# Decoder layer, gated delta rule: the output projection as three fp32r products of split halves

## The chip, the cores and the metric

One Trainium2 chip, one core of it. The time is device microseconds (us) of one execution of the whole program; lower is better.

## What is computed

A decoder layer on x of 16 batches x 128 positions x 256 features, float32. Its first part, a gated delta rule with 16 key heads and 32 value heads, takes most of the time, and its last lines are what the change touches:

```python
    o = o.transpose(1, 0, 2, 3)                   # output of the recurrence, B x S x 32 x 128
    og = o * jax.nn.silu(z)
    var = jnp.mean(og * og, axis=-1, keepdims=True)
    on = og * jax.lax.rsqrt(var + EPS) * norm_w
    return on.reshape(B, S, VAL_DIM) @ w_out      # 4096 x 256
...
    x = _layernorm(x + _L0_attn_ref(x, ...), axis=-1)
    x = _layernorm(x + _L0_xattn_ref(x, ctx_512, ctx_512), axis=-1)
    x = _layernorm(x + _L0_ffn_ref(x, ...), axis=-1)
```

## The kernel before

The recurrence is solved in closed form per batch and head. The work of the first part is cut into 64 steps: a step is one key head (so two value heads) and four batches, 8 pairs of batch and value head. One loop over n = 0 to 72 writes the instructions of all five engines, and it runs several stages of a software pipeline at once: stage 1 works on step n (projection of keys and queries, products of keys), the v stage on vn = n - 7, the third stage on m = n - 8 (the triangular inverse, deltas, outputs, gate), the fourth on k = n - 9 (norm, transpose and output projection). There is no scheduler: each engine runs what stands in its block in the order written, and counts of semaphores are all that ties the engines together. SP (SyncE) issues all transfers, in one order too.

What TensorE does in one pass of the loop, in order, with the lines of the profile: z_proj(m, 0) (L1326 to L1328 with 256 columns, fp32r); the 32x32 products u1 (L1504), which wait for the gate of the step before; q_norms (L1358); z_proj(m, 1); the small products L1517 and L1524; v_proj of vn, two banks (L1326 to L1328 with 512 columns); u2 of four pairs (L1537); the key products of step n (L1548, 4 of them, fp32); u2 and tt128 of the other four pairs (L1555 and L1456); on_tr(k, 0) and on_tr(k, 1), the eight transposes of the normed output into banks 4 and 5 (L1434); four more tt128 (L1456); out_proj(k, 0) and out_proj(k, 1) (L1451); deltas (L1469); kq_proj of n + 1 (L1326 to L1328 with 512 columns), which waits for the last convolution tap of v; the transposes of v (L1585); outputs (L1485).

VectorE, in the same pass: taps 2 and 3 of the convolution of keys and queries for step n (tap 1 stands at the end of the pass before; all are L897), the scalar of q_norms (L1131), a stretch of the inverse (L913 to L980), the taps 1 and 2 of v (L897), the four products of step n (L1100), tap 3 of v (L897), a stretch of the inverse, the diagonals (L1159), y_add(k), which adds the output projection out of banks 7 and 6 to Y (L1110), a stretch of the inverse, the two gates of m (L1115), tap 1 of n + 1. The 32x32 inverses are made for four steps together, in 41 operations; a generator hands them out in portions whose sizes the code sets (`pump(room)`). So the passes differ by n mod 4: in this text a pass is called of kind 0, 1, 2 or 3 by it. An inverse begins in a pass of kind 0 and ends in one of kind 3.

ScalarE: copies of u1 (L742), squares of the gated output (L688), SiLU of keys and queries (L748), copies L752 and L756, SiLU of z (L681), the copies v_tap3 with tap 0 of v (L669), the copies of u2 (L784, two halves), in kind 3 the copy of the inverse into another order (L794), on_T(k, 0) and on_T(k, 1), which bring the transposed normed output from banks 4 and 5 to the tile DL (L675), the copy L799, and later SiLU of v (L806), deltas (L812), kq_tap3 (L658) and v (L821). In kind 3 on_T(k, 0) stands before L794 and on_T(k, 1) behind it. GpSimd: the norm of step m, whose last instruction scales SZ (L578); then L554, the decay masks (L494, L498), the low halves of split weights (L472) and scale_wo, which multiplies w_out of a key head by the norm's weight (L485).

Projections from x are already made as three products of halves: a float32 operand is split into a high half, rounded to fp32r, and a low half, the rest (split_hi on ScalarE, split_lo on GpSimd), and high x high, high x low and low x high are added (`three`, L1326 to L1328). The output projection instead is one plain float32 product per pair:

```python
for b in range(2):
    for v in range(2):
        t = pe.matmul(ps(7 - i, b * 256, [[1, 256]]), at(on_buf(k), (4 * i + 2 * b + v) * 128, [[1, 128]]),
                      at(WO, (k // 4 % 2) * 512 + v * 256, [[1, 256]]), start=(v == 0), stop=(v == 1))
t.then_inc(sem["out_mm"], 1)
```

It shows as two instructions per product in the profile, 16 per step. Banks 4 and 5 are written in turn by z_proj, on_tr, deltas and the transposes of v. After the 64 steps come cross attention and the experts, by tables of steps; the output projections of the last two steps stand at their beginning.

## Time and profile before

| | us |
|---|---|
| median of 3 runs | 2288.58 |
| lowest and highest | 2284.19, 2304.11 |
| the profiled execution | 2284.63 |
| its span, first to last instruction | 2282.7 |

Rows of the profile give the start in us from the span's beginning, the duration, the engine, the line, the operation, what it writes and reads, how many instructions are merged, and in brackets the idle time of the engine before it with what ended that. PE is TensorE (PEld its weight loads), DVE VectorE, ACT ScalarE, POOL GpSimd. A merged row's duration reaches to the end of its last instruction, and instructions overlap a little, so the cost of a row to its engine is read from its start to the next row's start.

### The profile page before, as it was taken

What the parts mean: (1) busy time and instruction counts of PE and PEld (TensorE: products, weight loads), DVE (VectorE), ACT (ScalarE), POOL (GpSimd) and SP (SyncE); (2) the same over time, 40 slices, a digit from 0 to 9 for tenths busy, and PEclk for the clock granted to TensorE, in tenths of its full rate; (3) what the DMA queues carried; (4) which work ended last, traced back from release to release, by engine and by line L of the source; (5) the groups of instructions that cost most, each with busy time, mean ns of one, the idle gap of its engine ahead of it and who ended that gap; (6) DMA issues with size and microseconds to landing.
All of it is one profiled execution on the core that took longest, in us unless ns stands there. A gap on an engine that the chain in (4) does not pass through costs nothing.

```text
span 2282.7 us, 48904 instructions
## 1 busy us (share of the span) xinstructions
PE 2116.3 (93%) x18108; PEld 1754.0 (77%) x18108; DVE 1799.2 (79%) x3536; ACT 1508.3 (66%) x3585; POOL 858.5 (38%) x760
## 2 busy tenths in 40 slices
PE   4659999999999999999999999998888899999998
PEld 4448888888888888888888888887766466666677
DVE  6889797988979788897978989797324776767665
ACT  4536777767677777777777777775656766566632
POOL 1533344435344444434434443531333123223232
PEclk8769999999999999999999999999889999999999
DMA  3332223232232332223233222312143012221232
GB/s 76 92 71 48 74 51 80 55 70 66 49 86 47 72 63 62 66 57 82 42 76 74 48 67 59 74 34 55 56 130 132 1 47 93 102 93 59 90 135 97
DMA packets 274635, 161.54 MB, mean 71 GB/s; under 512 B 209352, under 2 KB 246752, under 8 KB 269280
## 3 DMA queue, kind: packets, MB, share of 16 engines
...
## 4 chain that ended last, share of the span: by engine, by line
PE 75%; DVE 11%; ACT 6%; issue 4%; DMA 2%; SPq 1%; POOL 1%; DVEq 0%; ACTq 0%; POOLq 0%
PE ps L1326 9%; PE ps L1451 9%; PE ps L1328 8%; PE ps L1327 8%; PE ps L1548 5%; PE ps L1485 5%; PE ps L1469 5%; PE ps L1704 4%; PE ps L1434 3%; PE ps L1358 2%; PE ps L1585 2%; PE ps L1504 2%; PE ps L1555 2%; ACT SC L844 1%; PE ps L1456 1%
## 5 line engine op out<-in xcount | busy, mean ns | idle before, releaser
L897 DVE SCALAR_TENSOR_TENSOR A<-ps,CW,A 128x508 f32<-128x508 f32 (+2 forms) x768 | 516.1, 735 | 115.7 <-ACT A L669 109.8
L571 POOL TENSOR_SCALAR SM<-SM 128x8 f32<-128x8 f32 x64 | 12.7, 198 | 891.8 <-ACT DL L688 891.8
L1451 PE MATMUL ps<-WO,DL 128*128 128x256 f32 x1008 | 243.4, 393 | 8.8 <-ACT TTF L799 8.8
L1326 PE MATMUL ps<-XH,WH 128*128 128x512 f32 x512 | 218.3, 426 | 25.5 <-DVE A L897 24.1
L1451 PEld LDWEIGHTS ps<-WO,DL 128*128 128x128 f32 x1008 | 189.1, 194 | 42.3 <-ACT DL L675 14.1
L1328 PE MATMUL ps<-XH,WL 128*128 128x512 f32 x512 | 205.1, 401 | 0.0
L1327 PE MATMUL ps<-XL,WH 128*128 128x512 f32 x512 | 204.5, 399 | 0.0
L688 ACT ACTIVATE DL<-SZ 128x128 f32<-128x128 f32 x512 | 152.3, 299 | 66.6 <-issue 42.0
L1115 DVE TENSOR_TENSOR SZ<-SZ,ps 128x512 f32<-128x512 f32 x128 | 86.2, 685 | 124.7 <-PE ps L1485 123.1
L844 ACT ACTIVATE SC<-ps,A 128x128 f32<-128x128 f32 x512 | 141.7, 386 | 51.9 <-DVE A L1231 51.3
L1100 DVE TENSOR_TENSOR BP<-ps,EB 128x512 f32<-128x512 f32 x256 | 158.3, 682 | 2.7 <-ACT EB L663 2.7
L1326 PE MATMUL ps<-WH,XH 128*128 128x256 f32 x512 | 156.7, 306 | 0.7 <-ACT VV L821 0.7
L1327 PE MATMUL ps<-WL,XH 128*128 128x256 f32 x512 | 145.5, 284 | 0.0
L1328 PE MATMUL ps<-WH,XL 128*128 128x256 f32 x512 | 145.2, 284 | 0.0
L494 POOL TENSOR_TENSOR EB<-EB,HJ 128x1024 f32<-128x1024 f32 x64 | 128.9, 2015 | 38.2 <-DMA EB<-decay_rows 38.2
L578 POOL TENSOR_TENSOR SZ<-SZ,SM 128x1024 f32<-128x1024 f32 x64 | 140.2, 2190 | 5.0
L1548 PE MATMUL ps<-A 128*128 128x256 f32 x512 | 133.9, 406 | 4.8 <-DVE SM L1131 3.4
L1326 PEld LDWEIGHTS ps<-XH,WH 128*128 128x128 f32 x512 | 99.1, 194 | 48.9 <-issue 15.4
L658 ACT ACTIVATE A<-ps,CW 128x512 f32<-128x512 f32 x128 | 86.3, 689 | 70.9 <-PE ps L1328 49.5
L1469 PEld LDWEIGHTS ps<-VV,TTF 128*128 128x128 f32 x1024 | 125.9, 194 | 4.9 <-ACT TTF L799 1.7
L1485 PE MATMUL ps<-DL,BP 128*128 128x128 f32 x1024 | 127.2, 278 | 0.7 <-DVE Y L1110 0.2
L1469 PE MATMUL ps<-VV,TTF 128*128 128x128 f32 x1024 | 126.5, 277 | 1.4 <-ACT TTF L799 1.4
...
## 6 DMA issues: line engine op xcount, KB each, us to landing
EB<-decay_rows SPq DMA_DIRECT2D x128, 256.0 KB, 4.8
...
x_blocks<-BP SPq DMA_DIRECT2D x256, 32.0 KB, 1.7
...
TTF<-tt_blocks SPq DMA_DIRECT2D x256, 32.0 KB, 1.9
...
```

What stands on the lines that cost most here:

```text
L578: pool.tensor_tensor(szp, szp, at(SM, C_RR, [[1, 8], [0, 128]]), ALU.mult).then_inc(sem["on"], 1)
L688: t = act.activation(at(DL, pr * 128, [[1, 128]]), at(SZ, (m % 2) * 1024 + pr * 128, [[1, 128]]), ACT.Square, accum_out=at(SM, C_SS + pr, ...
L844: t = act.activation(at(SC, i * 512 + h * 128, [[1, 128]]), ps(s_bank(a, i), h * 128, [[1, 128]]), ACT.Exp, bias=q(Q_MX + 4 * i + h, [[1, ...
L897: dve.scalar_tensor_tensor(acc, ps(i, 0, [[128, 4], [1, 128 - s]]), at(CW, tile * 4 + 3 - s, [[1, 1]]), acc, ALU.mult, ALU.add).then_inc(s ...
L1100: dve.tensor_tensor(slot(n, h * 1024 + v * 256, [[512, 2], [128, 2], [1, 128]]), ps(2 + h, 0, [[256, 2], [128, 2], [1, 128]]), at(EB, (n % ...
L1326: pe.matmul(out, sa, ma, start=(kt == 0), stop=False)
L1327: pe.matmul(out, sa, mb, start=False, stop=False)
L1328: return pe.matmul(out, sb_, ma, start=False, stop=(kt == 1))
L1451: t = pe.matmul(ps(7 - i, b * 256, [[1, 256]]), at(on_buf(k), (4 * i + 2 * b + v) * 128, [[1, 128]]), at(WO, (k // 4 % 2) * 512 + v * 256, ...
L1469: t = pe.matmul(ps(4 + i, j * 128, [[1, 128]]), at(TTF, pr * 128, [[1, 128]]), at(VV, pr * 128, [[1, 128]]), start=True, stop=True)
L1485: t = pe.matmul(ps(6 + i, j * 128, [[1, 128]]), slot(m, pr * 256 + 128, [[1, 128]]), at(DL, pr * 128, [[1, 128]]), start=True, stop=True)
L1548: t = pe.matmul(ps(2 + b // 2, (b % 2) * 256, [[1, 256]]), at(buf, b * 128, [[1, 128]]), at(buf, b * 128, [[512, 2], [1, 128]]), start=Tru ...
```

## The change

Four things are changed.

- out_proj becomes out_hi and out_lo. Of the transposed normed output, on_T on ScalarE writes the high half (fp32r, tile DLR, which lies on DL), and a new on_lo(k, i) on VectorE writes the rest into SZR (which lies on SZ): it reads bank 4 + i and DLR. TensorE makes 16 products with the high half (with the high and the low half of the weights) and then 8 with the low half.
- The weights are split once per key head: they are loaded into the slot of w_v in WR between two loads of w_v, scaled there by GpSimd, rounded by ScalarE (split_wo_hi) and their rest made by GpSimd (split_wo_lo), into a new tile WOR. Before, two slots of WO were filled by turns.
- on_tr(k, 0) stands before the key products instead of behind L1555, and on ScalarE on_T(k, 0) stands between the two copies of u2.
- Banks 4 and 5, and the next SiLU of z, are freed by on_lo and out_mm instead of on_T and on_tr.

```diff
                 def load_v(hk):
...
-                        sp.wait_ge(sem["lo_v"], hk)
+                        sp.wait_ge(sem["wo_lo"], hk)
...
                 def load_wo(hk):
-                    if hk >= 2:
-                        sp.wait_ge(sem["out_mm"], 2 * (4 * (hk - 2) + 3) + 2)
-                    sp.dma_start(at(WO, (hk % 2) * 512, [[256, 2], [1, 256]]),
+                    sp.wait_ge(sem["lo_v"], hk + 1)
+                    sp.dma_start(at(WR, W_V, [[256, 2], [1, 256]]),
...
-                    if 0 <= vn < NSTEP and vn % 4 == 1 and vn // 4 + 1 < HK:
-                        load_v(vn // 4 + 1)
...
+                    if n % 4 == 2 and 0 <= n // 4 - 1 < HK:
+                        load_wo(n // 4 - 1)
+                    if n % 4 == 0 and 0 < n // 4 - 1 < HK:
+                        load_v(n // 4 - 1)
...
+                def split_wo_lo(hk):
+                    pool.wait_ge(sem["wo_hi"], hk + 1)
+                    pool.tensor_tensor(at(WOR, 512, [[1, 512]]), at(WR, W_V, [[1, 512]]), at(WOR, 0, [[1, 512]]).bitcast(f32),
+                                       ALU.subtract).then_inc(sem["wo_lo"], 1)
...
+                def split_wo_hi(hk):
+                    act.wait_ge(sem["wo_scaled"], hk + 1)
+                    if hk:
+                        act.wait_ge(sem["out_mm"], 8 * hk)
+                    act.activation(at(WOR, 0, [[1, 512]]), at(WR, W_V, [[1, 512]]), ACT.Copy).then_inc(sem["wo_hi"], 1)
...
                     if s3:
-                        for i in range(2):
-                            act.wait_ge(sem["u2"], 2 * m + 1 + i)
-                            act.activation(at(U2, i * 256, [[1, 256]], 64, 64), ps(7, i * 256, [[1, 256]], 64, 64), ACT.Copy,
-                                           scale=-1.0).then_inc(sem["u2_sb"], 1)
+                        u2_copy(m, 0)
+                    if s4 and k < NSTEP - 1:
+                        on_T(k, 0)
+                    if s3:
+                        u2_copy(m, 1)
...
+                    if n % 4 == 0 and 0 <= n // 4 - 2 < HK:
+                        split_wo_hi(n // 4 - 2)
...
+                def on_lo(k, i):
+                    dve.wait_ge(sem["on_T"], 2 * k + 1 + i)
+                    dve.tensor_tensor(on_low(k, i * 512, 512), ps(4 + i), at(on_buf(k), i * 512, [[1, 512]]).bitcast(f32),
+                                      ALU.subtract).then_inc(sem["on_lo"], 1)
...
                     pump(1560)
+                    if s4 and k < NSTEP - 1:
+                        on_lo(k, 0)
                     if sv:
                         v_tap(vn, 1)
+                    if s4 and k < NSTEP - 1:
+                        on_lo(k, 1)
...
-                def out_proj(k, i):
+                def out_hi(k, i):
                     if k % 4 == 0 and i == 0:
-                        pe.wait_ge(sem["wo_scaled"], k // 4 + 1)
+                        pe.wait_ge(sem["wo_lo"], k // 4 + 1)
...
+                            for part in range(2):
+                                pe.matmul(ps(7 - i, b * 256, [[1, 256]]),
+                                          at(on_buf(k), (4 * i + 2 * b + v) * 128, [[1, 128]]),
+                                          at(WOR, part * 512 + v * 256, [[1, 256]]),
+                                          start=(b == 0 and v == 0 and part == 0), stop=False)
+
+                def out_lo(k, i):
+                    pe.wait_ge(sem["on_lo"], 2 * k + 1 + i)
+                    for b in range(2):
+                        for v in range(2):
+                            t = pe.matmul(ps(7 - i, b * 256, [[1, 256]]), on_low(k, (4 * i + 2 * b + v) * 128, 128),
+                                          at(WOR, v * 256, [[1, 256]]), start=False, stop=(b == 1 and v == 1))
                     t.then_inc(sem["out_mm"], 1)
+
+                def out_proj(k):
+                    out_hi(k, 0)
+                    out_hi(k, 1)
+                    out_lo(k, 0)
+                    out_lo(k, 1)
...
                     if m:
-                        pe.wait_ge(sem["on_T"], 2 * (m - 1) + 1 + i)
+                        pe.wait_ge(sem["on_lo"], 2 * (m - 1) + 1 + i)
...
+                    if s4 and k < NSTEP - 1:
+                        on_tr(k, 0)
                     if s1:
                         buf = kq_buf(n)
```

On VectorE, in the middle of a pass (here of kind 2), the program before has the inverse (L962, L967), then the taps of v (L897), the products of step n (L1100) and the last tap:

```order
L962 TENSOR_TENSOR TM<-X,TI 128x256
L897 SCALAR_TENSOR_TENSOR A<-ps,CW,A 128x4x127 x2
L897 SCALAR_TENSOR_TENSOR A<-ps,CW,A 128x4x126 x2
L1100 TENSOR_TENSOR BP<-ps,EB 128x2x256 x4
L897 SCALAR_TENSOR_TENSOR A<-ps,CW,A 128x4x125 x2
```

The same place in the changed program, where L984, L919 and L1122 are the lines called L962, L897 and L1100 before, and L1136 is on_lo:

```order
L984 TENSOR_TENSOR TM<-X,TI 128x256
L1136 TENSOR_TENSOR SZR<-ps,DLR 128x512
L919 SCALAR_TENSOR_TENSOR A<-ps,CW,A 128x4x127 x2
L1136 TENSOR_TENSOR SZR<-ps,DLR 128x512
L919 SCALAR_TENSOR_TENSOR A<-ps,CW,A 128x4x126 x2
L1122 TENSOR_TENSOR BP<-ps,EB 128x2x256 x4
L919 SCALAR_TENSOR_TENSOR A<-ps,CW,A 128x4x125 x2
```

One on_lo stands ahead of the first tap of v and one ahead of the second.

On ScalarE, in a pass of kind 3, before (L669 is v_tap3, L784 the copies of u2, L675 on_T, L794 the copy of the inverse):

```order
L669 ACTIVATE A<-ps,CW 128x512
L784 ACTIVATE U<-ps 64x256 x2
L675 ACTIVATE DL<-ps 128x512
L794 ACTIVATE TM<-TI 128x32x32
L675 ACTIVATE DL<-ps 128x512
L799 ACTIVATE TTF<-ps 64x8x64
```

And now (L679 is v_tap3, L695 the copies of u2, L685 on_T, L814 the copy of the inverse):

```order
L679 ACTIVATE A<-ps,CW 128x512
L695 ACTIVATE U<-ps 64x256
L685 ACTIVATE DLR<-ps 128x512
L695 ACTIVATE U<-ps 64x256
L814 ACTIVATE TM<-TI 128x32x32
L685 ACTIVATE DLR<-ps 128x512
L819 ACTIVATE TTF<-ps 64x8x64
```

The first on_T moved between the two copies of u2; the second stays behind the copy of the inverse.

On TensorE, between v_proj and deltas, before (L1537, L1555 and L1456 are u2 and tt128, L1548 the key products, L1434 the transposes of the normed output, L1451 the output projection):

```order
L1537 MATMUL ps<-TA,BP 64x64 x4
L1548 MATMUL ps<-A 128x256 x4
L1555 MATMUL ps<-TA,BP 64x64
...
L1456 MATMUL ps<-TTF,U 64x64
L1434 MATMUL ps<-IDN,SZ 128x128 x8
L1456 MATMUL ps<-TTF,U 64x64 x4
L1451 MATMUL ps<-WO,DL 128x256 x8
L1469 MATMUL ps<-VV,TTF 128x128 x8
```

And now (in the same sequence L1586, L1599, L1606, L1505, with L1467 the transposes and L1485, L1494 the products with the high and the low half):

```order
L1586 MATMUL ps<-TA,BP 64x64 x4
L1467 MATMUL ps<-IDN,SZ 128x128 x4
L1599 MATMUL ps<-A 128x256 x4
L1606 MATMUL ps<-TA,BP 64x64
...
L1505 MATMUL ps<-TTF,U 64x64
L1467 MATMUL ps<-IDN,SZ 128x128 x4
L1505 MATMUL ps<-TTF,U 64x64 x4
L1485 MATMUL ps<-WOR,DLR 128x256 x16
L1494 MATMUL ps<-WOR,SZR 128x256 x8
L1518 MATMUL ps<-VV,TTF 128x128 x8
```

Four of the eight transposes moved ahead of the key products, and 8 float32 products became 24 in fp32r.

## Rows read from the trace of the kernel before

**Rows 1.** The page, chain that ended last: share of the span by engine.

```profile
PE 75%; DVE 11%; ACT 6%; issue 4%; DMA 2%; SPq 1%; POOL 1%; DVEq 0%; ACTq 0%; POOLq 0%
```

**Rows 2.** Windows: length, busy us (instructions) of PE, PEld, DVE, ACT, POOL; granted clock; DMA.

```profile
198.00:1545.00 1347.00, 1324.92 (x13032) 1156.18 (x13030) 1182.43 (x2260) 988.29 (x2340) 578.83 (x485) 1.00 0.28 63
1545.00:1760.00 215.00, 180.91 (x1755) 154.82 (x1754) 95.73 (x166) 129.96 (x367) 69.65 (x78) 0.89 0.31 98
```

**Rows 3.** Waits from 198 to 1545 us: total us, times, longest.

```profile
PE ps L1504 <- DVE SZ L1115: 11.6, 14, 0.8
DVE SZ L1115 <- PE ps L1485: 90.0, 56, 4.8
DVE A L897 <- ACT A L669: 52.9, 15, 4.2
```

**Rows 4.** Timeline of VectorE over four passes, kinds 2, 3, 0 and 1.

```profile
902.65 1.28 DVE L1115 TENSOR_TENSOR SZ<-SZ,ps 128x512 f32<-128x512 f32 x2
903.85 3.99 DVE L897 SCALAR_TENSOR_TENSOR A<-ps,CW,A 128x508 f32<-128x508 f32 x6
...
914.02 2.69 DVE L897 SCALAR_TENSOR_TENSOR A<-ps,CW,A 128x508 f32<-128x508 f32 x4
...
927.60 3.99 DVE L897 SCALAR_TENSOR_TENSOR A<-ps,CW,A 128x508 f32<-128x508 f32 x6
...
937.16 2.70 DVE L897 SCALAR_TENSOR_TENSOR A<-ps,CW,A 128x508 f32<-128x508 f32 x4
...
942.15 1.39 DVE L897 SCALAR_TENSOR_TENSOR A<-ps,CW,A 128x500 f32<-128x500 f32 x2
...
951.17 0.69 DVE L1115 TENSOR_TENSOR SZ<-SZ,ps 128x512 f32<-128x512 f32 x1 [4.76 <-PE ps L1485]
...
952.67 3.99 DVE L897 SCALAR_TENSOR_TENSOR A<-ps,CW,A 128x508 f32<-128x508 f32 x6
...
960.67 2.72 DVE L897 SCALAR_TENSOR_TENSOR A<-ps,CW,A 128x508 f32<-128x508 f32 x4 [3.95 <-ACT A L669]
...
975.35 0.69 DVE L1115 TENSOR_TENSOR SZ<-SZ,ps 128x512 f32<-128x512 f32 x1 [1.44 <-PE ps L1485]
...
976.85 3.99 DVE L897 SCALAR_TENSOR_TENSOR A<-ps,CW,A 128x508 f32<-128x508 f32 x6
...
1001.40 1.27 DVE L1115 TENSOR_TENSOR SZ<-SZ,ps 128x512 f32<-128x512 f32 x2
1002.59 0.74 DVE L897 SCALAR_TENSOR_TENSOR A<-ps,CW,A 128x508 f32<-128x508 f32 x1
```

**Rows 5.** Timeline of TensorE, pass of kind 2: first and last of eleven z products; the output projection.

```profile
905.82 0.28 PE L1327 MATMUL ps<-WL,XH 128*128 128x256 f32 x1
...
907.01 0.28 PE L1328 MATMUL ps<-WH,XL 128*128 128x256 f32 x1
...
915.99 3.72 PE L1451 MATMUL ps<-WO,DL 128*128 128x256 f32 x16
```

**Rows 6.** Timeline of ScalarE, GpSimd and TensorE in the pass of kind 3.

```profile
936.69 0.38 ACT L784 ACTIVATE U<-ps 64x256 f32<-64x256 f32 x1
...
939.71 2.04 ACT L794 ACTIVATE TM<-TI 128x1024 f32<-128x1024 f32 x1
941.53 0.65 ACT L675 ACTIVATE DL<-ps 128x512 f32<-128x512 f32 x1
...
934.11 2.95 POOL L578 TENSOR_TENSOR SZ<-SZ,SM 128x1024 f32<-128x1024 f32 x1
...
935.99 1.99 PE L1548 MATMUL ps<-A 128*128 128x256 f32 x8
...
938.52 1.09 PE L1434 MATMUL ps<-IDN,SZ 128*128 128x128 f32 x8
...
946.28 0.48 PE L1326 MATMUL ps<-XH,WH 128*128 128x512 f32 x1
```

**Rows 7.** Timeline of ScalarE, pass of kind 0: the first copy of u2.

```profile
961.33 0.38 ACT L784 ACTIVATE U<-ps 64x256 f32<-64x256 f32 x1
```

68 lines of the change are left out of this document (34 added, 34 removed).

## The prediction, made before the changed kernel ran

> **What bounds the kernel now.** I read the chain that ended last first: TensorE holds 75% of it, VectorE 11% [rows 1]. So TensorE is the engine to shorten, but a second one is near. The windows say how near. From 198 to 1545 us, 55 passes of the loop (n = 9 to 63, 24.5 us each), TensorE is busy 1324.92 of 1347 us at a granted clock of 1.00, VectorE 1182.43, that is 88% [rows 2]. An average does not tell whether 12% of idle time can take new work, so I read the waits next. TensorE waits for the gate of VectorE 14 times, once in four passes, and VectorE has two waits that recur: for outputs (56 times, up to 4.8 us) and for v_tap3 (15 times) [rows 3]. The timeline shows where these lie [rows 4]. From the gate's end at 976.85 (kind 1) to the next at 1002.59 VectorE works 25.74 us; 903.85 to 927.60 (kind 2) is the same with 23.75, and it is still working when kind 3 starts. It idles 4.76 us at the end of kind 3, 3.95 in the middle of kind 0 and 1.44 at its end. The passes take 25.74, 23.75, 25.07 (927.60 to 952.67) and 24.18 us, together 98.74. So kinds 1 and 2 are bound by VectorE, or by both; only kind 0 and the end of kind 3 have room, and the idle times can't be lent to another pass, since the inverse is spread by fixed rooms.
>
> **The products on TensorE.** Before, 16 instructions take 3.72 us. A z product has the new form, fp32r with 256 columns: eleven of them start from 905.82 to 907.01, 0.119 us apart, and one lasts 0.28. So 24 take 23 x 0.119 + 0.28 = 3.02 us [rows 5]: 0.70 less per step, 44 us over 63 steps, if TensorE's work set the time everywhere.
>
> **The subtraction on VectorE.** on_lo reads a bank and a tile and writes 512 columns, as a gate does: two gates start at 902.65 and the next work at 903.85 [rows 4], 0.60 each, 1.2 us per pass. In kind 1 nothing hides it, and TensorE's saving can't show there, since the gate that ends the pass waits for VectorE's own queue: +1.2. Bounds per subtraction: 0.34 (half of a tap, four of which take 2.69) and 0.69 (a gate alone, at 951.17); I take 0.60, the back-to-back gates.
>
> **The new wait on VectorE.** on_lo(k, 0) stands ahead of tap 1, on_lo(k, 1) ahead of tap 2. Both wait for ScalarE's on_T, that for TensorE's transposes, and these for GpSimd's norm. Behind them are queued all taps of v, for which kq_proj waits, then the products of step n, y_add and the gates. What the wait costs depends on the kind:
>
> - Kind 2: before, tap 1 starts at 914.02, without a wait. on_T(k, 0) has to follow v_tap3 and the first copy of u2, so it can be late for on_lo by up to its own 0.6; I take 0.1 beyond the 1.2, so +1.3. In kind 1 I take no wait.
> - Kind 3: GpSimd ends the norm at 934.11 + 2.95 = 937.06, TensorE is at the place of the first transposes at 935.99 [rows 6]. They wait 1.1 us (before, they ran at 938.52 and waited for nothing), take half of 1.09, and the copy 0.6: on_lo(k, 0) starts at 938.4 instead of tap 1 at 937.16. The key products and L1555 follow; they took from 935.99 to 938.5, so they end at 940.2. The second copy of u2 (0.38 and 0.2 of hand-over) ends at 940.8, and then stands L794, 941.53 - 939.71 = 1.82 us, to 942.6. Only then on_T(k, 1), to 943.2. VectorE wants it at 940.4 (on_lo 0.6, two taps at 2.70 / 4 each): 2.9 us of waiting. Tap 3 ended at 943.54 and ends now 1.2 + 2.9 + 1.2 = 5.3 us later, at 948.8. kq_proj started at 946.28, so 2.7 us hide, and the rest, 2.6 us, is on the path. out_lo and deltas are earlier than that.
> - Kind 0: tap 1 waited until 960.67. Now on_lo(k, 0) waits for the copy of u2 (961.33 + 0.38) [rows 7] and on_T (0.6): 962.4, 1.8 later. on_T(k, 1) comes behind the key products, L1555, the other transposes and the second copy: by the spans of kind 3, about 4.3 us after the place of the first transposes at 961.1, so at 965.4. VectorE is there at 964.3, 1.1 us more. With the two subtractions 4.1 us, of which the idle time of 1.44 and 0.2 before the gates takes 1.6: +2.45 on the path.
>
> Per four passes: 1.2 + 1.3 + 2.6 + 2.45 = 7.55 us. The 55 passes are 14 of each of kinds 1, 2 and 3 and 13 of kind 0: 14 x 5.1 + 13 x 2.45 = 103.3 us.
>
> **What lies beside other work.** ScalarE gets one rounding of weights in four passes, 512 columns like L675 with its 0.65 us [rows 6], in kind 0, where it is 73% busy over the stretch [rows 2]; GpSimd, 43% busy, gets one subtraction more, at a place where it then waits for the squares anyway. The load of w_out now shares a slot with w_v. Its queue on SP is passed by the load of w_v, which moves behind store_x and load_rows and has two passes until it is split: cost nothing; if that cover failed, the first use in kind 1 would wait for a transfer, a few us in four passes. The early transposes are worth something where TensorE waited for the copy of u2; in kinds 0 to 3 these gaps are not on the path any longer.
>
> **Passes 64 to 71 and behind.** No key work is left, VectorE has 55% idle and the granted clock is 0.89 [rows 2]. Passes 64 and 65 still have an inverse: +2.5 and +1.2. In the six behind them I take 0.8 us less each, the 0.70 and a part of a wait. Sum -1, bounds -8 and +5. The last two projections lose 0.7 each and gain two subtractions and their hand-over: zero.
>
> **Sum.** 103.3 - 1 = 102 us. The profiled execution took 2284.63, so 2387. The median of the runs shown, 2288.58, stands 4 us above it; this is less than my steps are good for, and I leave the forecast at 2387. The least sure terms are the hand-overs of kinds 3 and 0. If they cost half, it is 35 us less (2352); if kinds 1 and 2 each wait 0.5 us more, 14 more, and 0.2 us of hand-over on each of the two links in kinds 3 and 0 makes 11 more, 2412.
>
> **Rivals.**
>
> *VectorE's idle time absorbs it, TensorE sets the time, and the kernel gets faster.* For it: TensorE is 98% busy and has 75% of the chain; VectorE idles 4.76 + 3.95 + 1.44 = 10.15 us in four passes, and needs 4.8 more. Against it: the idle time lies in kinds 3 and 0, and kinds 1 and 2 have none. This decides the sign if an on_lo takes under some 0.3 us and comes without a wait. Then 63 x 0.70 = 44 less: 2240.
>
> *Only the subtractions count.* on_T comes in time, or the delays of kinds 3 and 0 are hidden by the idle times of 4.76, 3.95 and 1.44 us. For it: these are larger than 1.2. Against it: the two waits of 2.9 and 1.8 follow from the order on ScalarE. Then 14 x 2.5 = 35, with 1 us each for the hand-overs 62: 2320 to 2347, middle 2335.
>
> *TensorE's clock falls.* With the delays TensorE is busy about 91% of the loop instead of 98. In the stretch where it is busy 84% the granted clock is 0.89 (a mean of stretches at 2.4 and at 1.2 GHz), in the loop 1.00 [rows 2]. If the loop's fell to 0.95, 5% of 1325 us are 66, half of it behind VectorE's work: 33 more, 2420. The gaps I work out are near 1 us each, while the waits of 2 to 5 us are what the slower stretch has.
>
> The Trainium skill, TensorE: Matmul & The Clock Gate, Part 1, says that the gate passes fewer clock pulses when the array has been less busy of late; the trace agrees in these two stretches, and by that rule the last rival would be what happens.
>
> *It does not move the time (within 1%).* Gains on TensorE and delays on VectorE cancel: about 2290. Nothing in the sum of kinds 1 and 2 speaks for it.
>
> **How the numbers follow.** Forecast 0.62; only the subtractions 0.22; clock 0.06; absorbed and faster 0.06; no change 0.04. A difference of over 1% is about what a measurement of this kernel can tell from none. Faster by over 1%: 0.05; within 1%: 0.05; slower by over 1%: 0.90. The range holds the forecast with its bounds and the middle and upper part of the second case: 2335 to 2415, with some 0.8.
>
> **What would show it.** Right: VectorE at 92% or more in the loop with hardly an idle gap in kinds 1 and 2; four passes in about 106 us; a wait of on_lo for on_T of about 3 us in kind 3 and 2 in kind 0; a wait of TensorE for the transposes' input of 1 us in kind 3, and for tap 3 at kq_proj; 24 products in 3.0 us. Wrong: the pitch of the products is not 0.12; four passes under 101 us; VectorE's wait for on_T is under a microsecond; on_lo takes much less than 0.6 us; or a granted clock under 0.98 in the loop.

## The result, and the profile after

| | before | changed |
|---|---|---|
| median of 4 runs, us | 2287.94 | 2458.74 |
| lowest and highest | 2284.19, 2304.11 | 2450.74, 2474.07 |
| the profiled execution | 2284.63 | 2450.74 |
| its span | 2282.7 | 2449.0 |
| mean granted clock of the span | 0.968 | 0.937 |

Here the kernel before has a fourth execution, of 2287.31 us.

The changed kernel takes 1.074 times the time before, with an interval from 1.0666 to 1.0814. The forecast was 2387 and its range ended at 2415: the direction was right, the size was not. Predicted were 102 us more, and the profiled executions differ by 166.

I read after in the order of before. First the page's chain by engine, which answers to [rows 1]:

```profile
PE 40%; DVE 32%; issue 14%; ACT 6%; POOL 4%; DMA 2%; SPq 1%; DVEq 0%; ACTq 0%; POOLq 0%
```

TensorE's share fell from 75% to 40%, VectorE's rose from 11% to 32%. The windows answer to [rows 2]. The first has the same limits as there, the second is the stretch of the 55 passes n = 9 to 63, which is now 191.17 to 1714.03. The columns are the length, busy us and instructions of PE, PEld, DVE, ACT and POOL, the granted clock and the DMA share and rate:

```profile
198.00:1545.00 1347.00, 1236.36 (x12022) 1078.97 (x12021) 1151.43 (x2118) 893.88 (x2099) 536.23 (x449) 0.95 0.26 57
191.17:1714.03 1522.86, 1395.74 (x13625) 1218.72 (x13626) 1302.54 (x2386) 1004.57 (x2377) 600.46 (x504) 0.95 0.25 56
```

The 55 passes took 1358.69 us before (185.75 to 1544.44, read in the same way) and take 1522.86: 164.2 more, so nearly the whole loss of 166 is in them. What stands ahead of them takes 5.4 us more and what stands behind them 3.3 less. VectorE's work there grew from 1194.48 to 1302.54 us. Two subtractions a pass at their pitch of 0.60 us (316.14 to 316.74 below) are 110 x 0.60 = 66 of these 108 us; 42 are of something else. TensorE is busy 1395.74 of 1522.86 us, that is 92%, where it was 98%. And the granted clock is 0.95, where it was 1.00. Both are the first signs of what the prediction left out.

The waits from 198 to 1690 us (who waits, for whom, total us, times, longest) answer to [rows 3]:

```profile
DVE SZR L1136 <- ACT DLR L685: 171.0, 58, 5.7
...
PE ps L1359 <- DVE A L919: 36.3, 54, 1.8
...
PE ps L1553 <- DVE SZ L1142: 33.2, 41, 1.1
...
PE ps L1534 <- DVE Y L1132: 27.0, 27, 1.6
DVE SZ L1142 <- PE ps L1534: 22.2, 26, 1.5
```

VectorE's largest wait is the new one, on_lo for on_T. TensorE waits for the taps in 54 passes, and for the gate 41 times instead of 14. VectorE's wait for outputs, which was 90.0 us, is down to 22.2: that reserve is used up.

Where it lies is told by the four kinds of passes, measured on the timeline of VectorE from the end of one gate to the end of the next, in the 55 passes:

| kind | passes | before, sum | after, sum | more | before, one at full clock | after, one at full clock |
|---|---|---|---|---|---|---|
| 1 | 14 | 360.6 | 420.9 | 60.3 | 25.75 | 30.1 |
| 2 | 14 | 334.1 | 367.2 | 33.1 | 23.76 | 24.96 |
| 3 | 14 | 348.7 | 391.8 | 43.1 | 25.07 | 27.17 |
| 0 | 13 | 315.4 | 342.9 | 27.5 | 24.17 | 26.37 |

Kind 1 has over a third of the loss, and the prediction gave it the least, 1.2 us a pass. Its timeline of VectorE and of GpSimd, pass n = 13:

```profile
302.55 3.99 DVE L919 SCALAR_TENSOR_TENSOR A<-ps,CW,A 128x508 f32<-128x508 f32 x6
...
307.42 3.00 DVE L957 TENSOR_TENSOR TM<-X,TI 128x512 f32<-128x512 f32 x2
...
312.52 3.70 DVE L973 TENSOR_TENSOR TM<-TI,UT 128x512 f32<-128x512 f32 x2
316.14 0.68 DVE L1136 TENSOR_TENSOR SZR<-ps,DLR 128x512 fp32r<-128x512 f32 x1
316.74 1.39 DVE L919 SCALAR_TENSOR_TENSOR A<-ps,CW,A 128x508 f32<-128x508 f32 x2
318.05 0.68 DVE L1136 TENSOR_TENSOR SZR<-ps,DLR 128x512 fp32r<-128x512 f32 x1
```

```profile
305.67 0.20 POOL L581 TENSOR_SCALAR SM<-SM 128x8 f32<-128x8 f32 x1 [7.22 <-ACT DL L709]
...
307.95 1.92 POOL L588 TENSOR_TENSOR SZ<-SZ,SM 128x1024 f32<-128x1024 f32 x1
...
312.26 1.91 POOL L503 TENSOR_TENSOR EB<-EB,HJ 128x1024 f32<-128x1024 f32 x1
```

The same place before, VectorE and then GpSimd, in the pass that begins at 976.85 in [rows 4]:

```profile
981.71 1.42 DVE L935 TENSOR_TENSOR TM<-X,TI 128x512 f32<-128x512 f32 x2
...
985.34 2.14 DVE L951 TENSOR_TENSOR TM<-TI,UT 128x512 f32<-128x512 f32 x2
```

```profile
982.70 2.19 POOL L578 TENSOR_TENSOR SZ<-SZ,SM 128x1024 f32<-128x1024 f32 x1
...
986.89 2.36 POOL L494 TENSOR_TENSOR EB<-EB,HJ 128x1024 f32<-128x1024 f32 x1
```

Two pairs of products of the inverse, which the change doesn't touch, took 1.42 and 2.14 us and take 3.00 and 3.70: 3.1 us more. In exchange GpSimd's two instructions are shorter, 1.92 and 1.91 instead of 2.19 and 2.36. All of these read two tiles in SBUF. Who starts first has changed: before, the second product of the first pair starts at 981.71 + 0.71 = 982.42 and GpSimd 0.28 us behind it; now GpSimd starts at 307.95 and the product would have started at 308.13. From the start of the taps GpSimd's instruction comes after 5.85 us before and after 5.40 now. The pass ahead is now bound by VectorE up to its gate, so TensorE stands ready when the gate ends. Its rows, before (taps from 976.85) and now (taps from 302.55):

```profile
977.49 0.69 PE L1504 MATMUL ps<-TA,BP 32*32 32x32 f32 x32
302.78 0.69 PE L1553 MATMUL ps<-TA,BP 32*32 32x32 f32 x32 [1.13 <-DVE SZ L1142]
```

Before, VectorE's two gates waited for TensorE (1.44 and 0.2 us, [rows 4]), and TensorE came to u1 0.64 us after the taps began. Now the gates wait for nothing, TensorE waits for them, u1 starts after 0.23 us, and the chain u1, squares, norm comes earlier by 0.4. That is a reading. Experiments e5, e6 and e12 test whether the order of the starts makes the 3.1 us; e4 bears on what moved GpSimd's start.

The Trainium skill, SBUF — State Buffer, section "Who interferes with whom", says that a VectorE instruction with two inputs in SBUF and a GpSimd one that reads SBUF exclude each other, and that the order in which they start, not what they are, decides who is held up. The trace agrees in both directions: 1.6 us on VectorE for each pair, 0.3 to 0.45 on GpSimd.

The new products are what they were forecast to be. TensorE, pass of kind 2, answers to [rows 5]:

```profile
344.73 2.18 PE L1485 MATMUL ps<-WOR,DLR 128*128 128x256 f32 x16
346.74 1.12 PE L1494 MATMUL ps<-WOR,SZR 128*128 128x256 f32 x8
347.70 1.95 PE L1518 MATMUL ps<-VV,TTF 128*128 128x128 f32 x16
350.00 0.50 PE L1359 MATMUL ps<-XH,WH 128*128 128x512 f32 x1 [0.34 <-DVE A L919]
```

From 344.73 to 347.70, where deltas start, is 2.97 us, for 3.55 before (915.99 to 919.54). So the change saves 0.58 a step on TensorE, and behind it TensorE stands for 0.34 us and waits for the taps.

The hand-overs of kind 3, in the pass that begins at 467.58, VectorE, then TensorE; they answer to [rows 4, 6]:

```profile
478.54 0.69 DVE L1136 TENSOR_TENSOR SZR<-ps,DLR 128x512 fp32r<-128x512 f32 x1 [1.31 <-ACT DLR L685]
...
483.20 0.69 DVE L1136 TENSOR_TENSOR SZR<-ps,DLR 128x512 fp32r<-128x512 f32 x1 [2.67 <-ACT DLR L685]
```

```profile
483.79 1.19 PE L1485 MATMUL ps<-WOR,DLR 128*128 128x256 f32 x8 [1.40 <-ACT TTF L819]
...
488.38 0.47 PE L1359 MATMUL ps<-XH,WH 128*128 128x512 f32 x1 [0.65 <-DVE A L919]
```

And of kind 0, VectorE, in the pass that begins at 386.22; they answer to [rows 4, 7]:

```profile
395.94 0.69 DVE L1136 TENSOR_TENSOR SZR<-ps,DLR 128x512 fp32r<-128x512 f32 x1 [5.66 <-ACT DLR L685]
...
398.87 0.69 DVE L1136 TENSOR_TENSOR SZR<-ps,DLR 128x512 fp32r<-128x512 f32 x1 [0.93 <-ACT DLR L685]
```

In kind 3 the second on_lo starts 15.62 us into the pass (forecast: 943.2 - 927.60 = 15.6); in kind 0 the two start after 9.72 and 12.65 us (forecast 9.7 and 12.7).

Last the clock. Windows of a pass of kind 2 (332.72 to 357.67) and of three stretches of the pass of kind 3 behind it:

```profile
357.67:360.30 2.63, 2.48 (x48) 2.47 (x49) 2.63 (x6) 2.56 (x13) 0.00 (x0) 1.00 0.66 163
360.40:367.00 6.60, 6.60 (x63) 5.47 (x62) 6.50 (x7) 4.88 (x13) 5.61 (x5) 0.50 0.00 0
367.00:386.31 19.31, 17.24 (x137) 15.06 (x136) 12.07 (x29) 15.42 (x26) 8.12 (x8) 0.99 0.35 87
332.72:357.67 24.95, 24.11 (x248) 21.15 (x248) 24.51 (x44) 15.55 (x43) 10.75 (x9) 1.00 0.20 31
```

From 360.4 to 367.0 TensorE runs at 0.50, the level of 1.2 GHz, although it is busy throughout, and was busy 24.11 of 24.95 us in the pass ahead. The z products stand 0.12 us apart until 360.39 and 0.21 after it. This pass took 28.64 us instead of 27.17, and 8 of the 14 passes of kind 3 took 28.5 or 28.6. In kind 2 such a stretch makes 27.92 of 24.96, and 6 of the 14 passes have one. In kind 1 it costs nothing (30.05 us at a clock of 0.89 as at 1.00), because VectorE sets the time there.

So the 164 us are, by these rows:

| cause | us |
|---|---|
| kind 1, VectorE and GpSimd exclude each other, 14 x 3.1 | 43 |
| kinds 1 and 2, the two subtractions, 14 x (1.2 + 1.2) | 34 |
| kind 3, hand-over, 14 x 2.1 | 29 |
| kind 0, hand-over, 13 x 2.2 | 28 |
| lower clock: kind 2, 367.2 - 14 x 24.96 = 18; kind 3, 391.8 - 14 x 27.17 = 11 | 29 |
| sum | 163 |

The first is in none of the prediction's cases; the last was a rival there and no term of the sum.

### The profile page after: what moved, and what is told of

It is laid out like the page before. It is cut to its first block, busy times and chain, and to the rows that moved or that the text cites. A ratio compares the mean times of both kernels' runs of the same rounds, so it can differ in the third digit from the quotient of the medians.

```text
span 2449.0 us, 50103 instructions
## 1 busy us (share of the span) xinstructions
PE 2170.6 (89%) x18620; PEld 1806.6 (74%) x18620; DVE 1916.8 (78%) x3664; ACT 1518.3 (62%) x3601; POOL 874.4 (36%) x776
## 3 DMA queue, kind: packets, MB, share of 16 engines
q1 hardware_dynamic: 274400, 158.41, 25.4%
## 4 chain that ended last, share of the span: by engine, by line
PE 40%; DVE 32%; issue 14%; ACT 6%; POOL 4%; DMA 2%; SPq 1%; DVEq 0%; ACTq 0%; POOLq 0%
DVE A L919 8%; PE ps L1359 7%; PE ps L1361 5%; PE ps L1360 5%; DVE BP L1122 5%; PE ps L1750 4%; PE ps L1534 3%; DVE TM L973 2%; DVE TM L957 2%; PE ps L1599 2%; DVE SZ L1142 2%; ACT SC L866 2%; PE ps L1391 2%; DVE TI L977 1%; DVE UT L961 1%
## 5 line engine op out<-in xcount | busy, mean ns | idle before, releaser
L919 DVE SCALAR_TENSOR_TENSOR A<-ps,CW,A 128x508 f32<-128x508 f32 (+2 forms) x768 | 520.4, 734 | 11.0 <-ACT A L668 5.6
L1359 PE MATMUL ps<-XH,WH 128*128 128x512 f32 x512 | 237.3, 464 | 60.6 <-DVE A L919 60.1
L1136 DVE TENSOR_TENSOR SZR<-ps,DLR 128x512 fp32r<-128x512 f32 x126 | 86.5, 687 | 243.5 <-ACT DLR L685 242.5
L1360 PE MATMUL ps<-XL,WH 128*128 128x512 f32 x512 | 219.4, 429 | 0.0
L1361 PE MATMUL ps<-XH,WL 128*128 128x512 f32 x512 | 218.2, 426 | 0.0
L826 ACT ACTIVATE A<-A 128x1024 f32<-128x1024 f32 x64 | 67.9, 1061 | 209.1 <-DVE A L919 209.1
L1485 PE MATMUL ps<-WOR,DLR 128*128 128x256 f32 x1008 | 144.0, 294 | 20.9 <-ACT TTF L819 20.9
L1122 DVE TENSOR_TENSOR BP<-ps,EB 128x512 f32<-128x512 f32 x256 | 158.4, 681 | 3.2 <-ACT EB L673 3.2
L1361 PE MATMUL ps<-WH,XL 128*128 128x256 f32 x512 | 155.8, 304 | 0.0
L1534 PE MATMUL ps<-DL,BP 128*128 128x128 f32 x1024 | 128.0, 278 | 27.6 <-DVE Y L1132 27.6
L1485 PEld LDWEIGHTS ps<-WOR,DLR 128*128 128x128 f32 x1008 | 128.3, 195 | 27.8 <-ACT DLR L685 23.5
L1534 PEld LDWEIGHTS ps<-DL,BP 128*128 128x128 f32 x1024 | 119.3, 192 | 36.2 <-issue 36.0
L503 POOL TENSOR_TENSOR EB<-EB,HJ 128x1024 f32<-128x1024 f32 x64 | 123.0, 1922 | 43.2 <-DMA EB<-decay_rows 43.2
L1599 PE MATMUL ps<-A 128*128 128x256 f32 x512 | 126.0, 389 | 7.1 <-DVE SM L1158 5.7
L1361 PEld LDWEIGHTS ps<-XH,WL 128*128 128x128 f32 x512 | 108.0, 211 | 27.1
```

What stands on the lines that cost most here:

```text
L503: pool.tensor_tensor(ap3, ap3, at(HJ, 4 * g * 32 + 2 * hk, [[1, 2], [32, 4], [0, 128]]), ALU.add).then_inc(sem["dec"], 1)
L919: dve.scalar_tensor_tensor(acc, ps(i, 0, [[128, 4], [1, 128 - s]]), at(CW, tile * 4 + 3 - s, [[1, 1]]), acc, ALU.mult, ALU.add).then_inc(s ...
L1122: dve.tensor_tensor(slot(n, h * 1024 + v * 256, [[512, 2], [128, 2], [1, 128]]), ps(2 + h, 0, [[256, 2], [128, 2], [1, 128]]), at(EB, (n % ...
L1359: pe.matmul(out, sa, ma, start=(kt == 0), stop=False)
L1360: pe.matmul(out, sa, mb, start=False, stop=False)
L1361: return pe.matmul(out, sb_, ma, start=False, stop=(kt == 1))
```

## The experiments

Where no number of runs is given, a run is one execution; the kernel before ran beside it on the same chip, and its time stands in brackets. Four executions of the changed kernel lie 23 us apart (2450.74 to 2474.07), so a difference smaller than that between two single executions proves nothing by itself; there the passes at full clock decide, most of which repeat to 0.1 us within a kernel. The loop's passes are read as in the table above. In the changed kernel deltas, outputs and gates are L1518, L1534 and L1142; a few lines more in front move these by as many.

**e1_late_tr: the early transposes undone.**

```diff
                         u2_copy(m, 0)
-                    if s4 and k < NSTEP - 1:
-                        on_T(k, 0)
                     if s3:
...
+                    if s4 and k < NSTEP - 1:
+                        on_T(k, 0)
...
-                    if s4 and k < NSTEP - 1:
-                        on_tr(k, 0)
                     if s1:
...
                     if s4 and k < NSTEP - 1:
+                        on_tr(k, 0)
                         on_tr(k, 1)
```

> The changed kernel with the early transposes alone undone: the eight transposes of the normed output behind the second block of u2 again, both copies of u2 ahead of on_T(k, 0). Theory (the hand-over from ScalarE to VectorE costs): on_T(k, 0) comes later, so on_lo(k, 0) waits 1 to 2 us in every kind of pass; 2451 grows to 2500 or more. Rival (it is the early transposes that cost, since TensorE waits for GpSimd's norm in kind 3): the time falls below 2440 and TensorE's waits in kind 3 go.

Measured: 2506.31 us [2282.24]. Kind 0 takes 27.9 us instead of 26.4 and kind 2 29.0 instead of 26.2 in the mean, at a clock of 0.90; kind 1 takes 31.0 for 30.1. Against the expectation kind 3 gets shorter, 26.1 for 28.0. On balance the early transposes help: of the four parts this one takes 45 us off the 55 passes. VectorE waits 207.5 us for on_T from 198 to 1600 us, against 171.0 from 198 to 1690 in the changed kernel.

**e2_pool_shift: GpSimd delayed ahead of the norm, meant for kind 1.**

```diff
                         pool.wait_ge(sem["ss"], 2 * m + 2)
+                        if n % 4 == 1:
+                            for c in (21, 22):
+                                pool.tensor_scalar(at(SM, c, [[1, 1]]), at(SM, C_PH, [[1, 1]]), 1.0, 1.0, ALU.mult, ALU.mult)
```

> The changed kernel with two one-column instructions of GpSimd (about 0.28 us each) ahead of its norm in passes of kind 1 alone, so that all its work there comes about 0.5 us later. Theory (in kind 1 four products of the inverse on VectorE meet instructions of GpSimd that started first, and stand still for about 1.6 us twice): the pass of kind 1 falls from 30.0 to about 27 us, L957 x2 from 3.0 to 1.4 us, and the time by about 14 x 3 = 42 us to 2410. Rival (kind 1 is long because of waits for TensorE or ScalarE): no change within 10 us, or a little more time.

Measured: 2448.78 us [2282.24], kind 1 as in the changed kernel at 30.08. The delay stood in the wrong place: the norm that the code of pass n writes runs behind the gate that ends pass n, so in the time of pass n + 1, and the two instructions fell into kind 2, which went from 24.96 to 25.92 at full clock. The expectation for kind 1 was not tested. It shows one thing by the way: GpSimd later by half a microsecond in kind 2 costs 1 us there.

**e3_filler: more work for TensorE ahead of the wait for the taps.** deltas(m, 1) is made twice, with the same result, in kinds 1 to 3.

```diff
-                def deltas(m, i):
+                def deltas(m, i, times=1):
...
-                    for j in range(4):
+                    for j in [j for _ in range(times) for j in range(4)]:
...
-                    if s3:
+                    if s3 and n % 4 == 0:
                         deltas(m, 1)
+                    elif s3:
+                        deltas(m, 1, 2)
```

> The changed kernel with the four products of deltas(m, 1) made twice in passes of kinds 1, 2 and 3, same values, about 0.9 us more work of TensorE ahead of its wait for the last tap of v. Theory (part of the loss is the granted clock, which falls where TensorE has gaps): the clock of the loop rises from 0.95 to 0.98 or more, passes of kind 2 are all near 25.0 instead of 28 in every second, and the time falls by 20 to 35 us to about 2420. Rival (the clock's dips are only a sign, VectorE sets the time anyway, or more products just cost): no change or up to 20 us more.

Measured: 2469.35 us [2282.24], granted clock 0.94 from 198 to 1525 us, where the changed kernel has 0.95; kind 1 30.05, kind 2 26.8, kind 3 28.3 in the mean. TensorE was busy 1242 us of these 1327 instead of 1220, and the clock did not rise, so the theory fell that filling the gaps at the taps brings it back. It was not a test of all gaps: in kind 1 TensorE still waits for the taps up to 0.9 us (1.8 without the filler) and 1.5 us for y_add, and in kind 3 1.4 us for a copy of ScalarE.

**e4_no_low: without on_lo and the low half's products.** The output projection lacks the term low half of the normed output x high half of the weights; banks and stores are freed by on_T and out_hi instead.

```diff
                     pump(1560)
-                    if s4 and k < NSTEP - 1:
-                        on_lo(k, 0)
                     if sv:
                         v_tap(vn, 1)
-                    if s4 and k < NSTEP - 1:
-                        on_lo(k, 1)
...
                     out_hi(k, 1)
-                    out_lo(k, 0)
-                    out_lo(k, 1)
```

> The changed kernel without the low half of the normed output: no on_lo on VectorE and no products with it, so two of the three products are left (the output loses that term). Theory (the whole loss comes from on_lo, by its work, its waits and what these set off): about 2250 to 2290, not slower than the kernel before, with a loop clock of 1.00 and passes of 25.7, 23.6, 24.5 and 22.6 us. Rival (the split of weights, the shared slot or the early transposes cost as well): above 2320.

Measured: 2315.52 us [2282.24], clock 0.949. All the work and the waits of on_lo are gone, and the kernel is still 33 us slower than before. Its 55 passes take 46 us more: 43 are in kind 1, 14 in kind 3 and 4 in kind 2, and kind 0 gives back 14. Kind 1 takes 28.8 us, 3.1 more than before, with both pairs of products at 3.00 and 3.69. So those 3.1 us are not on_lo's. Here too the gates at the end of kind 0 wait for nothing, u1 starts 0.23 us after the taps begin and GpSimd's norm after 5.42. With on_lo gone, what takes the wait of the gates away must be another part of the change, on TensorE the shorter products or the earlier transposes; no run separates them. The miss led to the reading of who starts first.

**e5_shift_k1: the delay of e2 in the right pass.** n % 4 == 0 in place of 1, the same two instructions.

```diff
                         pool.wait_ge(sem["ss"], 2 * m + 2)
+                        if n % 4 == 0:
+                            for c in (21, 22):
+                                pool.tensor_scalar(at(SM, c, [[1, 1]]), at(SM, C_PH, [[1, 1]]), 1.0, 1.0, ALU.mult, ALU.mult)
```

> The changed kernel with two one-column instructions of GpSimd ahead of its norm where it runs in a pass of kind 1 (the run before had put them into kind 2 by mistake). The work of GpSimd there comes 0.56 us later, so that it starts behind the second L957 of VectorE and not 0.2 us ahead of it. Theory (who starts first holds the other up): L957 x2 falls from 3.0 to 1.4 us, L973 x2 from 3.7 to 2.1, the pass of kind 1 from 30.05 to about 27.0, the time to 2449 - 14 x 3 = 2407. Rival (these instructions are slow for another reason, such as where the tiles lie): the pass stays at 30.

Measured: 2410.51 us [2281.98]. Work was added and the kernel became 40 to 48 us faster than the changed one. VectorE and GpSimd in a pass of kind 1 that begins at 395.55:

```profile
400.42 1.42 DVE L960 TENSOR_TENSOR TM<-X,TI 128x512 f32<-128x512 f32 x2
...
404.03 2.14 DVE L976 TENSOR_TENSOR TM<-TI,UT 128x512 f32<-128x512 f32 x2
```

```profile
401.32 2.28 POOL L591 TENSOR_TENSOR SZ<-SZ,SM 128x1024 f32<-128x1024 f32 x1
```

GpSimd's instruction comes 5.77 us into the pass instead of 5.40, behind VectorE's second product (5.58), and the pairs are back at 1.42 and 2.14. Kind 1 takes 27.0 us at full clock, the forecast's 25.75 + 1.2. Of its 14 passes nine have a low clock now (28.2 to 31.4 us), so that the mean is 28.7: once VectorE no longer covers it, the clock costs time there too.

**e6_no_low_shift: e4 and the delay of e5 together.** It leaves out the same term as e4.

> The kernel without the low half (no on_lo, two products) with the same 0.56 us of delay of GpSimd in kind 1. Theory: its pass of kind 1 falls from 28.8 to about 25.8 us and the time from 2315.5 to about 2273, below the kernel before: so everything that is left of the loss there was the meeting of VectorE and GpSimd. Rival: 2315, and the shared slot or the early transposes cost the rest.

Measured: 2268.88 us [2281.98], 46.6 us less than e4 by the delay alone; kind 1 25.82. So without the subtractions (and with 16 products instead of 24), and with GpSimd behind VectorE, the change is worth 13 us against the kernel before. None of them is in the 55 passes, which take 1359.04 us for 1358.69: kind 0 gives back 14.8, kind 3 takes 12.5 more (TensorE waits there for the norm, up to 1.5 us), and kinds 1 and 2 take 2.6 more. The gain lies in the passes 64 to 71, 181.9 us for 196.3. What was paid for, the time on TensorE, was worth little even without its price. No cost of the split of the weights or of the shared slot shows in this kernel's kinds 1 and 2, but neither was undone by itself.

**e7_lo_later: the hand-overs.** on_lo(k, 0) behind tap 2 of v and on_lo(k, 1) between the products of step n, and the copy of the inverse on ScalarE behind on_T(k, 1) and the copy that follows it (this part is not shown).

```diff
-                    if s4 and k < NSTEP - 1:
-                        on_lo(k, 0)
                     if sv:
                         v_tap(vn, 1)
-                    if s4 and k < NSTEP - 1:
-                        on_lo(k, 1)
...
+                    if s4 and k < NSTEP - 1:
+                        on_lo(k, 0)
                     if s1:
                         products(n, 0)
+                    if s4 and k < NSTEP - 1:
+                        on_lo(k, 1)
                     if s1:
```

> The changed kernel with on_lo(k, 0) behind tap 2 of v and on_lo(k, 1) between the two halves of the products, and ScalarE's copy of the inverse behind on_T(k, 1) and the copy of tt128. The same work, without the two hand-overs on the path. Theory: passes of kind 3 fall from 28.0 to about 25.4 and of kind 0 from 26.4 to about 24.0, kinds 1 and 2 stay at 30.05 and 25 (VectorE's work); the time falls by 14 x 2.6 + 13 x 2.4 = 68, to about 2380, and the waits of VectorE for on_T vanish. Rival (the waits only moved, what is behind them is late anyway): above 2420.

Measured: 2369.88 us [2281.98]. VectorE doesn't wait for on_T any more; kind 0 takes 24.08 us (24.17 before the change), kind 3 26.3. Instead TensorE waits for on_lo and, where the transposes now come first, for the norm; from 198 to 1600 us:

```profile
PE ps L1494 <- DVE SZR L1136: 51.2, 32, 2.7
...
PE ps L1467 <- POOL SZ L588: 19.3, 18, 1.5
```

**e8_lo_later_late_tr: e7 with e1.**

> As the run before, with the early transposes undone as well. Theory: with on_lo later nothing needs them; kind 3 loses TensorE's wait of about 1 us for GpSimd's norm, the others are equal; within 15 us of the run before, rather below it. Rival (the early transposes are needed for any version with on_lo): 40 us or more above it.

Measured: 2377.09 us [2281.98]. Kind 3 gets to 24.79 us, kind 0 goes to 25.29. Early transposes are good in kind 0 and bad in kind 3, where the norm isn't ready, and with on_lo later they are worth 3 us of the 55 passes, not 45 (7 us of the whole, which is less than single executions differ).

**e9_all_waits and e15_all_waits_timed: what was found, together.** e7, the delay of e5, and the first transposes and their copy late in kind 3 alone; e15 is the same kernel, timed.

```diff
-                    if s4 and k < NSTEP - 1:
+                    if s4 and k < NSTEP - 1 and n % 4 != 3:
                         on_tr(k, 0)
...
+                    if s4 and k < NSTEP - 1 and n % 4 == 3:
+                        on_tr(k, 0)
```

> The changed kernel with on_lo later, GpSimd 0.56 us later in kind 1, and the early transposes undone in kind 3 alone. Theory (the three causes add up): from 2370 less 14 x 3.0 for the meeting in kind 1 and 14 x 1.5 for TensorE's wait in kind 3: about 2307, passes of 27.0, 25.0, 24.8 and 24.1 us. What is left over the kernel before, 25 us, is then the work of on_lo in kinds 1 and 2. Rival (one wait was hidden behind another): above 2335.

> The changed kernel with on_lo later, GpSimd later in kind 1 and late transposes in kind 3 again, this time timed. Theory (what is left over the kernel before is the work of on_lo in kinds 1 and 2 alone, about 14 x (1.2 + 1.0) us less what TensorE saves elsewhere): 1.0 to 1.4% over the kernel before, with an interval that excludes 1. Rival (the one look flattered or hid something else): equal to it, or over 2%.

Measured: e9 2312.18 us [2290.86], e15 a median of 2330.97 us (2311.95 to 2333.34, 4 runs), 1.0172 times the kernel before, interval 1.013 to 1.0214. This is above the 1.0 to 1.4% that was expected of e15, though the interval reaches down to 1.3%. Kinds 1, 2, 3 and 0 take 27.0, 24.7, 24.7 and 24.1 us in e9. By the medians this form gives back 128 of the 171 us, and it stays slower than before. What is left at full clock is kind 1 with its 1.2 us and kind 2 with 1.0, 14 x 2.2 = 31 us, less what kinds 3 and 0 gain.

The two profiles of this one kernel differ by 21 us, and nearly all of it goes with the clock. Windows of e9 and then of e15:

```profile
198.00:1525.00 1327.00, 1263.16 (x13075) 1115.28 (x13074) 1205.90 (x2295) 968.76 (x2281) 584.32 (x511) 0.99 0.27 62
```

```profile
198.00:1525.00 1327.00, 1273.46 (x12878) 1124.37 (x12876) 1176.89 (x2257) 957.58 (x2249) 577.82 (x505) 0.97 0.27 62
```

In e15 every pass of kind 2 has a stretch at the low level (0.87 in the mean) and takes 26.3 us for 24.74: 14 x 1.56 = 22 us. The five executions took 2312 us twice, at a mean clock of the span of 0.963 and 0.958, 2333 twice, at 0.941 and 0.943, and 2328.64 once, at 0.946.

**e10_rebalanced and e11_before_rebalanced: the inverse's room moved from kinds 1 and 2 to kind 0,** in e9 and in the kernel before.

```diff
-                    pump(2500)
-                    pump(1560)
-                    if sv:
-                        v_tap(vn, 1)
                     if n % 4 == 0 and 4 <= n <= NSTEP:
                         under_way.append(inverse(n // 4 - 1))
+                    pump({0: 2400, 1: 1300, 2: 1300, 3: 2500}[n % 4])
+                    if n % 4:
+                        pump(1560)
+                    if sv:
+                        v_tap(vn, 1)
```

> The run before this with 2400 units of the inverse taken out of kinds 1 and 2 (1200 each) and made in kind 0, where VectorE waits about 4 us for v_tap3. Theory (what is left is VectorE's work in kinds 1 and 2): passes of kind 1 fall by about 1.4 us to 25.6, kind 2 to 24.1, time about 2280, equal to the kernel before. Rival (the moved instructions meet GpSimd's anew, or the inverse is late in kind 0): 2300 or more.

> The kernel before, output projection in float32, with the same move of the inverse into kind 0. Theory (kind 1 is bound by VectorE in the kernel before already): kind 1 falls from 25.75 to about 24.4, kinds 2 and 3 near 24.2 and 24.8; time 2282 - 14 x 1.4 = about 2262. Rival (TensorE binds all of it): 2282 within 8.

Measured: 2340.75 and 2341.16 us [2290.86], both some 60 to 80 above what was expected. Kinds 1 and 2 shrink as planned (23.9 and 23.8 in e10), but kind 0 takes 30.4 and 28.9. The timeline of e10 in kind 0, VectorE and then GpSimd, shows the same exclusion on small products:

```profile
372.01 1.89 DVE L978 TENSOR_TENSOR TM<-TI,UT 128x32 f32<-128x32 f32 x2
...
374.19 3.37 DVE L962 TENSOR_TENSOR TM<-X,TI 128x64 f32<-128x64 f32 x4
```

```profile
371.73 1.90 POOL L591 TENSOR_TENSOR SZ<-SZ,SM 128x1024 f32<-128x1024 f32 x1
...
374.56 1.04 POOL L563 TENSOR_TENSOR Q<-A 128x512 f32<-128x512 f32 x1
375.56 1.91 POOL L503 TENSOR_TENSOR EB<-EB,HJ 128x1024 f32<-128x1024 f32 x1
```

Elsewhere two products of 32 columns take 0.51 us and four of 64 columns 1.00. Here the first of the two products of 32 columns waits out the norm, which began 0.28 us before it. Of the four of 64 columns the third and the fourth wait out L563 and L503. Moving instructions of VectorE beside GpSimd's was not free here, small as they were.

**e12_before_dve_late: the kernel before, with 0.45 us more on VectorE in kind 1.** The clearest test of the omitted term, with nothing of the change in it.

```diff
                                           ALU.mult).then_inc(sem["nq"], 1)
+                    if n % 4 == 1 and s3:
+                        dve.tensor_reduce(at(SM, 21, [[1, 3]]), at(IDN, 0, [[0, 3], [1, 128]]), AX.X, ALU.max)
                     pump(2500)
```

> The kernel before with one more reduction on VectorE (128 x 384 elements to 3, about 0.45 us) in passes of kind 1, ahead of the inverse. Theory (who starts first holds the other up): GpSimd's norm now starts ahead of VectorE's second product; L935 x2 grows from 1.4 to 3.0 and L951 x2 from 2.1 to 3.7 us, the pass of kind 1 from 25.75 to 29.3, the time by 50 us to 2332, from 0.45 us of work. Rival: the work alone, 14 x 0.45 = 6 us, 2288.

Measured: 2346.77 us [2290.86]. VectorE in the pass that begins at 388.73:

```profile
392.70 0.54 DVE L1134 TENSOR_REDUCE SM<-IDN 128x3 f32<-128x384 f32 x1
...
394.05 3.00 DVE L935 TENSOR_TENSOR TM<-X,TI 128x512 f32<-128x512 f32 x2
```

And GpSimd, whose instruction starts 5.84 us into the pass as before, now ahead of VectorE's second product:

```profile
394.57 1.93 POOL L578 TENSOR_TENSOR SZ<-SZ,SM 128x1024 f32<-128x1024 f32 x1
```

One added instruction of half a microsecond makes kind 1 take 29.32 us for 25.75: 3.57 more, of which 3.1 are the two pairs. Its 55 passes take 62 us more than those of before: 50 are this, and 12 are passes of kinds 2 and 0: three of kind 2 and one of kind 0 now have a low clock, where the kernel before had one such pass.

**e13_before_600: the kernel before, with less moved.** As e11, with rooms of 600, 1900, 2500 and 2500 in kinds 0, 1, 2 and 3, timed.

> The kernel before with only the first 600 units of the inverse (six small instructions, 1.3 us) moved ahead of the taps in kind 0, and 600 less room in kind 1. Theory (kind 1 is bound by VectorE, and a short piece ends before GpSimd's norm is under way): kind 1 falls by 0.6 us to 25.1, kind 0 stays at 24.2, time 2282 to about 2274. Rival (the other phase of kind 1 makes VectorE and GpSimd meet anew, as the larger move did in kind 0): 2300 or more.

Measured: 2271.81 us (2271.51 to 2273.16, 4 runs), 0.9933 times the kernel before, interval 0.9917 to 0.995. Kind 1 takes 24.44 for 25.75, twice the fall that was expected, and no other kind grows by more than 0.15. It is faster than both kernels, if by less than 1% than the one before. Kind 1, bound by VectorE, was where the kernel before had something to give, not the output projection.

**e14_all_600: the same rooms in e9.**

> The changed kernel with on_lo later, GpSimd later in kind 1, late transposes in kind 3, and the same move of 600 units. Theory: kind 1 falls by 0.6 us from 27.0, time from 2312 to about 2304. Rival: the instructions meet anew, 2330 or more.

Measured: 2304.62 us [2287.5]. Kind 1 falls to 25.86, kind 2 is at 25.4 in the mean, with a low clock in 6 of its 14 passes. The change in its best form here stays behind the kernel before.

Who starts first, in six of these kernels, in us from the start of the taps in a pass of kind 1 (the second column is the start of the first product and 0.71 us):

| kernel | second product of the first pair could start | GpSimd's norm starts | first | the two pairs take |
|---|---|---|---|---|
| before | 5.57 | 5.85 | VectorE | 1.42, 2.14 |
| changed | 5.58 | 5.40 | GpSimd | 3.00, 3.70 |
| e4 | 5.59 | 5.42 | GpSimd | 3.00, 3.69 |
| e5 | 5.58 | 5.77 | VectorE | 1.42, 2.14 |
| e6 | 5.58 | 5.77 | VectorE | 1.42, 2.14 |
| e12 | 6.03 | 5.84 | GpSimd | 3.00, 3.69 |

## Why the prediction was right in direction and wrong in size

**Right: what binds.** That kinds 1 and 2 are bound by VectorE, and that TensorE's saving can't show there, holds: kind 2 rose by 1.2 (forecast 1.3), and the kernel without on_lo and with GpSimd behind VectorE (e6) gained nothing in the 55 passes, and 13 us in all where 44 were the whole saving. Its kinds 1 and 2 are in the sum no shorter than before.

**Right: TensorE.** 24 products take 2.97 us (forecast 3.02). The subtraction has a pitch of 0.60, as taken from the gates.

**Right: the hand-overs, step by step.** In kind 3 on_lo(k, 1) starts 15.6 us into the pass as forecast; kq_proj comes at 20.8 (488.38 - 467.58), for 18.7 before (946.28 - 927.60), so 2.1 us are on the path. The forecast had 2.6, because it let kq_proj wait for the whole of tap 3, which ends at 21.2, and TensorE starts 0.4 before that end. In kind 0 both starts are right to 0.1 us and the term is 2.2 for 2.45. Together these two were 68 us in the forecast and are 57. One wait of the prediction hardly came: TensorE was to wait about 1 us for the norm, ahead of the transposes of kind 3; from 198 to 1690 us it did so in one pass (1.5 us). In the pass from 467.58 it came to them just as the norm was done.

**The step that failed: kind 1, "nothing hides it: +1.2".** The time of the subtractions was right. What failed is the tacit step that the rest of VectorE's work keeps its durations, a term put at nothing without a reason. Kind 1 rose by 4.3 us: 1.2 of the subtractions and 3.1 of two pairs of products that GpSimd holds up, 43 us in all. e12 shows it with nothing of the change, e5 takes it away by adding work. The prediction itself used up the 1.44 and 0.2 us that the gates of kind 0 waited, and did not ask what starts earlier in the next pass once TensorE stands ready for them. The rows for it were there before: GpSimd's L578 took 2.95 us in kind 3 [rows 6] and 1.90 to 2.20 in the other kinds, and I took 2.95 as its price without asking what made it so.

**The second: the clock.** It stood among the rivals with a chance of 0.06 and a price of 33 us. The price was good, 29 us. The chance was too low, as far as one case tells: my argument against it was that gaps near 1 us are not enough, and the gaps of the changed kernel are indeed 0.3 to 1.8 us. The first step feeds this one: e12, with the 3.1 us in kind 1 and nothing else, has four passes at a low clock where the kernel before has one. The forecast named a clock under 0.98 as what would show it wrong, and it is 0.95. What sets it is open. Filling gaps at the taps (e3) did not restore it; taking the waits away did for the most part (e9, 0.99), and in the same kernel it came out at 0.97 (e15). The Trainium skill, TensorE: Matmul & The Clock Gate, Part 1, cited in the prediction, gives the direction, and the trace agrees with it: TensorE was busy 98% of the loop at a clock of 1.00 and is busy 92% at 0.95. Neither allows one to say for a schedule which clock it will get.

**The other rivals.** "VectorE's idle time absorbs it" fell, and in e7, where VectorE waits for nothing of on_T, the loop still stays slower. "Only the subtractions count" (35 us and up to 27 for hand-overs) was too small from both sides. With the forecast's other terms as measured (34 + 57 = 91 for 103) the range would have held; the 43 us of kind 1 alone carry the time to 2419, beyond it.

**The signs.** Four passes take 108.6 us at full clock and 110.7 in the mean, where about 106 were named. VectorE is busy 86% of the loop and not 92, because its waits grew (171.0 us for on_T) while the passes became longer. The waits for on_T, 2.67 us in kind 3 and in kind 0 5.66 us where 3.95 were waited before, and the 24 products are as named.
